# Inverse norms of the rotary attention in a six-layer stage: one logarithm, one exponential and a Newton step per token tile, in place of a power per chunk

## The reference, cut to what matters

```python
for i in range(DEPTH):                                   # 6 layers
    x = attn_layer(shift_tokens(x), Wqkv[i], q_scale[i], k_scale[i], Wo[i]) + x
    x = ffn_layer(shift_tokens(x), ...) + x

# attn_layer: 16 heads of 64
q, k, v = split(x @ Wqkv)
q = l2norm(q) * qs ; k = l2norm(k) * ksc                 # l2norm(t) = t / max(|t|, 1e-12)
q = q * cos * scale + rotate_half(q) * sin * scale
k = k * cos / scale + rotate_half(k) * sin / scale
out = local_attention(q, k, v)                           # windows of 32, looking one window back
```

## Time and profile before

| | |
|---|---|
| median of 3 runs | 2469.64 us (2464.82 to 2473.2) |
| span of the profiled execution | 2469.5 us |
| PE busy in the span | 1995.8 us (81%) |
| DVE | 1761.0 us (71%) |
| ACT | 1453.6 us (59%) |
| POOL | 1028.3 us (42%) |
| stage d | 1278.6 us to the end |

### The profile page before, as it was taken

One profiled execution on the slowest core, in us unless ns is written; L12 is line 12 of the kernel. 1 busy time (PEld: TensorE's weight loads), 2 busy tenths in 40 slices (PEclk: granted clock), 3 DMA queues, 4 the chain that ended last, 5 costly groups with the idle time before them and its releaser, 6 DMA issues. The chain is left out here.

```text
span 2469.5 us, 52904 instructions
## 1 busy us (share of the span) xinstructions
PE 1995.8 (81%) x18992; PEld 926.7 (38%) x18992; DVE 1761.0 (71%) x3039; ACT 1453.6 (59%) x2138; POOL 1028.3 (42%) x1009
## 2 busy tenths in 40 slices
PE   5647888888888888888847988988988988888886
PEld 3421222222222222222223554654554554555454
DVE  4736666676666666666658978878878877887794
ACT  4313556666555656555726766756757657666573
POOL 0011111111111111111039968858758767686680
PEclk9856889999899999888969998999999999999998
DMA  1022222222222222222010000000000000000000
GB/s 32 2 52 51 45 54 55 47 51 49 44 52 56 52 56 52 56 52 54 2 58 1 2 29 10 12 30 10 12 31 10 12 30 10 12 30 11 12 2 10
DMA packets 52105, 77.07 MB, mean 31 GB/s; under 512 B 10899, under 2 KB 45749, under 8 KB 48053
## 3 DMA queue, kind: packets, MB, share of 16 engines
q1 hardware_dynamic: 51317, 74.06, 13.0%
q10 hardware_dynamic: 576, 0.15, 0.0%
HBM read 47.70 MB, written 25.69 MB: 30 GB/s over the span
## 5 line engine op out<-in xcount | busy, mean ns | idle before, releaser
L902 DVE TENSOR_REDUCE ENM<-PM 128x1 f32<-128x512 f32 x1024 | 656.5, 685 | 335.9 <-PE PM L735 328.4
L832 ACT ACTIVATE EPT<-PA 128x1024 f32<-128x1024 f32 x512 | 520.0, 1021 | 212.0 <-PE PA L747 199.9
L735 PE MATMUL PM<-EKX,EQX 48*128 48x512 bf16 x1024 | 359.7, 414 | 177.0 <-DMA EKX<-e_park 91.0
L1216 POOL TENSOR_TENSOR DRN<-DRN,DHALF 128x8 f32<-128x8 f32 x192 | 364.5, 1899 | 7.4
L655 POOL CAST ENMP<-ENM 128x16 bf16<-128x16 f32 x64 | 12.6, 196 | 847.8 <-DVE ENM L902 847.8
L1214 POOL TENSOR_TENSOR DQR<-DR 128x512 f32<-128x512 f32 x192 | 244.2, 1272 | 246.9 <-DVE DR L1497 245.5
L735 PEld LDWEIGHTS PM<-EKX,EQX 48*128 48x128 bf16 x1024 | 83.6, 95 | 585.4 <-DVE ENM L902 404.1
L757 PE MATMUL PV<-EPT,EVP 128*32 128x512 f32 x2048 | 295.2, 651 | 0.9 <-ACT EPT L832 0.7
L747 PE MATMUL PA<-EQX,EKX 51*128 51x512 bf16 x1024 | 263.2, 404 | 5.2 <-DMA EQX<-EROWS 4.9
L1259 PE MATMUL PM<-DWQKV,DXS 128*128 128x512 f32 x384 | 216.6, 647 | 39.5 <-ACT XNT L1456 23.2
L1495 DVE TENSOR_TENSOR DR<-DRAW,DTAB 128x512 f32<-128x512 f32 x192 | 193.1, 1005 | 61.9 <-POOL DQR L1219 28.2
(11 more groups left out here) (204 smaller groups left out, 2930.8 us busy)
## 6 DMA issues: line engine op xcount, KB each, us to landing
e_park<-EPARTS SPq DMA_DIRECT2D x64, 192.0 KB, 2.9
EQX<-e_park SPq DMA_DIRECT2D x32, 384.0 KB, 5.6
EKX<-e_park SPq DMA_DIRECT2D x32, 384.0 KB, 9.2
DWQKV<-in_WqkvR SPq DMA_DIRECT2D x6, 1536.0 KB, 6.3
e_park<-EPARTS SPq DMA_DIRECT2D x64, 128.0 KB, 2.6
e_park<-EPARTS SPq DMA_DIRECT2D x64, 64.0 KB, 2.1
EQX<-EROWS SPq DMA_DIRECT2D x256, 3.0 KB
DWO<-in_WoR SPq DMA_DIRECT2D x6, 512.0 KB, 4.3
```

The lines of the kernel that those rows point to most:

```text
L735: pe.matmul(PM[:, r, :], lhsT=QX[64 * r:64 * r + KQ, b, hp, t * 128:(t + 1) * 128], rhs=KX[64 * r:64 * r + KQ, b, hp, :], start=True, stop ...
L832: s_.activation(PT[:, kt, pair * 2 * S:(pair + 1) * 2 * S], PA[:, 2 * pair:2 * pair + 2, :].rearrange("p a b -> p (a b)"), ACT.Exp, scale= ...
L902: v.tensor_reduce(NM[:, g % 2, t, j, 0:1], PM[:, r, :], AX.X, ALU.max, negate=True).then_inc(maxed, 1)
L1216: g.tensor_tensor(rn, rn, HALF[:, 0:8], ALU.pow).then_inc(rooted.sem, 1)
```

## The change

- The floor is no longer made per chunk. DVE's sums of squares of the four chunks of a tile go side by side into `SS` [128, 2, 32]. A new piece `norm` for tile k-1 stands in slot k at place 5, between `score` (place 0) and the first chunk (place 10; `pturn` at 9). DVE floors the 32 sums of each token in one instruction and multiplies them by -0.5; ACT takes the logarithm with scale -2 and then the exponential with scale -0.5, which gives a first value r of the inverse root; POOL does a Newton step, r(1.5 - 0.5 s r²), in four small instructions on 128x32.
- POOL's share of a chunk changes: in slot k it first multiplies chunk (k-1, c) by its inverse norms (L1229 of the changed kernel), then adds `R2` to chunk (k, c) in place (L1233). The multiplication is thus done one slot later than the addition. `QR` takes the place of `R1` and has six buffers.
- ACT loads one table set that has both the logarithm and the exponential at the start of the stage, and again after the last Gelu of each sequence. There are as many table loads in a layer as before.
- `HALF` shrinks to 128x4, a tile `THREE` of 1.5 is set once.

```diff
         if k in (0, TB):
             order.append((k, 1, "shift", k // TB))
+        if 1 <= k <= NT:
+            order.append((k, 5, "norm", k - 1))
...
+        QR, R2 = m.sb("DQR", [128, 6, 512]), m.sb("DR2", [128, 2, 512])
+        SS, RN = m.sb("DSS", [128, 2, 32]), m.sb("DRN", [128, 2, 32])
...
+                    elif name == "norm":
+                        ss, rn = SS[:, n % 2, :], RN[:, n % 2, :]
+                        pool.wait_ge(guessed.sem, guessed.at(layer, n))
+                        g.tensor_tensor(NEWT[:, :], rn, rn, ALU.mult).then_inc(newton.sem, 1)
+                        pool.wait_ge(newton.sem, newton.at(layer, 3 * n))
+                        g.tensor_tensor(NEWT[:, :], NEWT[:, :], ss, ALU.mult).then_inc(newton.sem, 1)
...
+                        g.tensor_tensor(rn, rn, NEWT[:, :], ALU.mult).then_inc(rooted.sem, 1)
+                    elif name == "proj":
                         k = 4 * n[0] + n[1]
...
-                        g.tensor_tensor(qr, r1, r2, ALU.add).then_inc(joined.sem, 1)
-                        pool.wait_ge(floored.sem, floored.at(layer, k))
-                        g.tensor_tensor(rn, rn, HALF[:, 0:8], ALU.pow).then_inc(rooted.sem, 1)
...
+                        if n[0]:
+                            qr, rn = QR[:, (k - 4) % 6, :], RN[:, (n[0] - 1) % 2, 8 * n[1]:8 * n[1] + 8]
+                            pool.wait_ge(joined.sem, joined.at(layer, k - 4))
+                            pool.wait_ge(rooted.sem, rooted.at(layer, n[0] - 1))
+                            g.tensor_tensor(qr.rearrange("p (h e) -> p h e", h=8), qr.rearrange("p (h e) -> p h e", h=8),
+                                            bc(rn, 2, [128, 8, DL]), ALU.mult).then_inc(roped.sem, 1)
+                        if n[0] < NT:
+                            pool.wait_ge(rotated.sem, rotated.at(layer, k))
+                            g.tensor_tensor(QR[:, k % 6, :], QR[:, k % 6, :], R2[:, k % 2, :], ALU.add).then_inc(joined.sem, 1)
...
+                    elif name == "norm":
+                        wait(floored, n)
+                        s.activation(LOGS[:, :], SS[:, n % 2, :], ACT.Ln, scale=-2.0).then_inc(logged.sem, 1)
+                        wait(logged, n)
+                        wait(roped, 4 * (n - 2) + 3)
+                        s.activation(RN[:, n % 2, :], LOGS[:, :], ACT.Exp, scale=-0.5).then_inc(guessed.sem, 1)
...
-                        wait(roped, k - 2)
+                        wait(turned, k - 6 if k >= 6 else -1)
                         v.tensor_tensor(r1, x, bc(tab[:, 0], 1, [128, 8, DL]), ALU.mult).then_inc(step, 1)
+                        wait(joined, k - 2)
...
-                        v.tensor_scalar(RN[:, k % 2, :], SS[:, k % 2, :], 1e-24, None, ALU.max).then_inc(floored.sem, 1)
+                    elif name == "norm":
+                        wait(summed, 4 * n + 3)
+                        v.tensor_scalar(SS[:, n % 2, :], SS[:, n % 2, :], 1e-24, -0.5, ALU.max, ALU.mult).then_inc(floored.sem, 1)
```

More of the change, by code:

```diff
@@ L1105, in stage_d @@
         MASK = m.sb("DMASK", [128, 2, DL])
-        HALF = m.sb("DHALF", [128, 8])
+        HALF = m.sb("DHALF", [128, TB])
         XS = m.sb("DXS", [128, B, W + S])
         RAW, SQ = m.sb("DRAW", [128, 2, 512]), m.sb("DSQ", [128, 2, 512])
-        R1, R2, QR = m.sb("DR1", [128, 2, 512]), m.sb("DR2", [128, 2, 512]), m.sb("DQR", [128, 4, 512])
-        SS, RN = m.sb("DSS", [128, 2, 8]), m.sb("DRN", [128, 2, 8])
+        QR, R2 = m.sb("DQR", [128, 6, 512]), m.sb("DR2", [128, 2, 512])
+        SS, RN = m.sb("DSS", [128, 2, 32]), m.sb("DRN", [128, 2, 32])
+        LOGS, NEWT, THREE = (m.sb(x, [128, 32]) for x in ("DLOGS", "DNEWT", "DTHREE"))
         QT = m.sb("DQT", [128, 2, HP, 128])
@@ L1194, in _ @@
                 g.memset(HALF[:, :], -0.5).then_inc(padded, 1)
+                g.memset(THREE[:, :], 1.5).then_inc(padded, 1)
                 g.memset(XS[:, :, :], 0.0).then_inc(padded, 1)
                 g.memset(KT[:, :, :, 0:W], 0.0).then_inc(padded, 1)
-                pool.wait_ge(padded, 3)
+                pool.wait_ge(padded, 4)
                 pool.wait_ge(const, 32)
-                pool.sem_inc(roped.sem, roped.credit)
+                for e in (roped, joined, rooted):
+                    pool.sem_inc(e.sem, e.credit)
                 def piece(layer, name, n):
@@ L1236, in _ @@
                     pe.sem_inc(e.sem, e.credit)
[L1237 removed]
+                pe.wait_ge(padded, 4)
                 def piece(layer, name, n):
@@ L1264, in proj @@
                             for i in range(4):
-                                mm = turn(m, pe, PX[:, i * 128:(i + 1) * 128], QR[:, k % 4, i * 128:(i + 1) * 128])
+                                mm = turn(m, pe, PX[:, i * 128:(i + 1) * 128], QR[:, (k - 4) % 6, i * 128:(i + 1) * 128])
                             mm.then_inc(turned.sem, 1)
@@ L1488, in piece @@
                         x = RAW[:, k % 2, :].rearrange("p (h e) -> p h e", h=8)
-                        r1, r2 = (r[:, k % 2, :].rearrange("p (h e) -> p h e", h=8) for r in (R1, R2))
+                        r1, r2 = (r.rearrange("p (h e) -> p h e", h=8) for r in (QR[:, k % 6, :], R2[:, k % 2, :]))
                         tab = TAB[:, 2 * (c // 2):2 * (c // 2) + 2, t, :]
@@ L1498, in piece @@
                         wait(squared, k)
[L1499 to L1501 removed]
+                        if c == 0:
+                            wait(rooted, n[0] - 2)
+                        v.tensor_reduce(SS[:, n[0] % 2, 8 * c:8 * c + 8], SQ[:, k % 2, :].rearrange("p (h e) -> p h e", h=8), AX.X, ALU.add).then_inc(summed.sem, 1)
+                    elif name == "norm":
+                        wait(summed, 4 * n + 3)
+                        v.tensor_scalar(SS[:, n % 2, :], SS[:, n % 2, :], 1e-24, -0.5, ALU.max, ALU.mult).then_inc(floored.sem, 1)
                     elif name == "score":
```

26 lines of the change are left out of this document (10 added, 16 removed).

## The result

The changed kernel takes 2766.9 us (median of 4 runs, 2763.8 to 2768.6), the kernel before 2470.5 (4 runs). The ratio is 1.1195, with a 95% interval from 1.1173 to 1.1216: slower by 12%. The forecast was 2767. The span of its profiled execution is 2765.0 us.

A forecast was written before the change was run, and what follows sets the result against it. PE was taken to bound plain slots, with 17.1 us of work. Losses of 180 (plain slots), 30 (slots 2, 3), 72 (7, 8) and 15 us (0, 1) made 297 us on 2469.5: 2767 us, range 2630 to 2870.

The forecast's parts named there:

- What bounds the kernel: Plain slots: PE is busy 17.10 of 17.10 us and bounds them, although the chain's shares point to POOL.
- POOL was the bound: Rival: relieving POOL removes waits in slots 2, 3, 7 and 8, saving 60 us, to 2410 us; faster had chance 0.04.
- the 1 us a plain slot: Plain slots: removing POOL's powers and DVE's small floors gains at most 1 us each, from 18.1 to 17.1 us.
- The chain: From the end of PE's scores through DVE's scores, floor, logarithm, exponential and Newton step to the first scaled chunk: 7.3 us.
- The stretch: PE idle before a slot's first chunk transposes, waiting for the norm and scaling: 5.5 us in each of slots 2 to 8.
- The sign that I had given: PE's timeline: 5 to 6 us idle before each slot's first transposes, released by POOL's scaling.
- Inside the slot: At later chunks PE waits for scalings that POOL does only after its additions: 2.5 us a slot, bounds 0 and 4.
- The clock: After the long idle time PE resumes at 1.2 GHz: 2.0 us a slot, from 1.8 to 4.2.
- The plain slot: 17.1 + 5.5 + 2.5 + 2.0 = 27.1 us, 9.0 more than 18.1; 180 us over 20 such slots.
- Slots 2 and 3: Layers 2 to 6: 14 of 20 us covered by waits and half clock already there; 6 us a layer, 30 us remain.
- Slots 7 and 8, 0 and 1: Slots 7 and 8 lose 12 us a layer, 72 in all; slots 0 and 1 lose 3 us, 15 in all.
- The table loads: On ACT: as many as before, at the end of the Gelus, and costing nothing.

The follow-up runs named there:

- run 2: The kernel before with its 192 powers on POOL turned into products, leaving the inverse norm out of the result: 2416.1 us, ratio 0.979.
- run 7: The changed kernel with each tile's norm behind the last chunk of its own slot and POOL scaling one chunk ahead of its additions: 2446.5 us, ratio 0.991.
- Run 1: The changed kernel with the norm placed ahead of the scores, which moved nothing in the first layer: 2633.6 us, ratio 1.067.
- run 8: The changed kernel with the norm ahead of the scores in all six layers, POOL's order left as it is: 2600.8 us, ratio 1.054.
- run 4: The changed kernel without the Newton step, POOL passing on the exponential's value: 2709.0 us, ratio 1.098.
- run 3: The changed kernel with five extra projections on PE in its wait before the first transposes of slots 2 to 7: 2726.1 us, ratio 1.105.
- run 5: The changed kernel with POOL scaling one chunk ahead of what it adds, norm still behind the scores: 2687.7 us, ratio 1.086.
- run 6: The changed kernel with the norm ahead of the scores in all six layers and POOL scaling one chunk ahead of its additions: 2455.9 us, ratio 0.994.

## Why the prediction was right, step by step

**What bounds the kernel.** Right. Of the two views, the window over the plain slot decided, not the chain's shares: run 2 took 305 us from POOL and left the plain slots alone. The 53 us that it did give lie where the rival "POOL was the bound" placed them, in slots 2, 3, 7 and 0 to 1, and near its size (60). Of the 1 us a plain slot that I allowed for the powers, run 2 shows nothing and run 7 half.

**The chain.** Forecast 7.3 us after the end of PE's scores, measured 6.95 (1884.51 to 1891.46). DVE's three took 3.74, as forecast, floor 0.17, logarithm and exponential 0.49 with their hand-over (0.5), the four Newton operations 1.31 from the first to the scaling (1.3), the scaling 1.09 to PE's start (1.1). Only the hand-overs were smaller, 0.15 us in all where I had 0.5. Runs 1 and 8 show that the scores ahead of the floor are the cause of the stretch, run 4 that its length counts about one for one.

**The stretch.** Forecast 5.5 us in slots 2 to 8. Measured in layers 2 to 6: 6.5 us in slot 2, 3.5 to 5.1 in slot 3, 3.8 in slot 4, 5.1 in slots 5 to 7, 5.9 in slot 8; in the plain slots of layer 1, 4.4 to 6.5. The mean of the 20 plain slots is 5.0. The sign that I had given, 5 to 6 us in each slot, is thus not met in slots 2 to 4.

**Inside the slot.** The mechanism was right, its size was not what this trace could show: 1.1 us where I had 2.5. The step that failed is the assumption that this wait adds to the stretch and to the clock's price. A part of it lies under the slow matmuls: in run 3, with the stretch there and the clock held, it is 2.0 us (0.85 and 1.18). Another lies under the stretch, in which DVE and POOL catch up: with the stretch gone, in run 8, the same order costs 0.45, 2.92 and 1.19 us.

**The clock.** From the first transposes to the second v projection PE needs 5.68 us in the slot shown (1891.46 to 1897.14), and 3.08 at full clock in run 7 (1939.27 to 1942.35), 2.6 us less. Over the 15 plain slots of layers 2 to 6 it is 4.44 to 5.81 us, 5.23 on average: 2.1 us for the clock, forecast 2.0. It falls to 1.2 GHz in every plain slot of the changed kernel. But three rows were too few to say when it falls: it had held after 2.39 us there, and in run 8 it falls behind a wait of 2.00 us in two layers and holds in three. Run 3 shows the mechanism by holding it off.

**The plain slot.** For the slot shown, 17.1 + 5.1 + 1.1 + 2.6 = 25.9, measured 26.2. The mean of all 20 is 26.35, forecast 27.1. Against the 18.6 of before, by the same instruction, it is 154 us, forecast 180: 26 too many, mostly the in-slot wait of 2.5 us that is 1.1.

**Slots 2 and 3.** Forecast 6 us a layer, 30 in all; measured 12.2 (65.3 for 53.1), 61 in all. I had counted 14 of 20 us as covered by idle time that was there. PE's wait of 4.63 us did shrink (to 1.3), but slot 2 also got a new one, 4.19 us in layer 3, larger than the 1.3 that I had put on one in-slot wait: the scaling stands behind the addition and behind the layer norm's power as well. I had asked what the moved scaling is queued behind among the additions only, and not what else POOL does between. Run 5, which puts the scaling ahead of both, gives slot 2 4.5 us back and so confirms the wait; it does not tell the power's part from the addition's.

**Slots 7 and 8, 0 and 1.** 76 and 10 us, forecast 72 and 15. The table loads, put at nothing, no run tests by themselves; run 7 has them all and is faster than the kernel before.

So the sum, 297 us forecast and 296 measured, hit better than its terms, and that is luck: 26 too many in the plain slots and 31 too few in slots 2 and 3 cancelled. What was right without luck is the shape: a first wait of some 5 us a slot, the clock lost behind it, and POOL relieved for next to nothing.

**Where the expectations missed.** Run 1 was expected at 2400 to 2470, as if the stretch were the whole loss. The two orders have to be mended together (run 6). Run 2 was expected to bring the plain slots to 17.1 to 17.5 us, and they stayed at 18.6. Run 3 gave 41 us for 70 to 85, and run 5 fell 12 us below its range: behind the first stands in part the in-slot wait, behind the second the later waits of slots 2 and 7.

## What to carry to other kernels

When a step is moved to where it is done once for several pieces, ask on each engine what its queue holds at the new place, everything and not only the same loop's work: here DVE's three score instructions, and POOL's additions and layer norm, turned 320 us less work into 296 us more time, and a change of places alone, with no instruction more or less, took the same program to 0.9% under the kernel before. Waits in series hide each other, so a cure tried alone shows less than it is worth; try them together before dropping one. And a term for idle stretches of PE of 4 to 5 us, as here, needs its second part, here some 2 us a slot, for the slow matmuls behind it; under these a later wait may hide.
